# Two edits to a one-core transformer kernel: preparation moved between the first three stages, and a query's squares folded before they are summed

## The chip, the cores and the metric

The kernel runs on one core of a Trainium2 chip. The metric is the device time of one execution in microseconds (us). The engines of the core are TensorE (PE in the rows, with PEld for its weight loads), VectorE (DVE), ScalarE (ACT), GpSimd (POOL) and SyncE (SP), which here only issues transfers. Each works through its own instructions in order, and they wait for one another on semaphores.

## The reference

`x` and `ctx` are [8, 256, 512] in float32. Two layers, each an attention and a feed-forward block, are added to `x`:

```python
x = x + xattn0(layernorm(x), ctx)      # one head of 512; keys = [ctx ; x wk], values = [ctx ; x wv]
x = x + ffn0(layernorm(x))             # ternary weights, 8-bit activations
x = x + xattn1(layernorm(x), ctx)      # 16 query heads of 128, 4 key/value groups, keys only from ctx
x = x + moe(layernorm(x))              # top 2 of 8 experts and a shared expert

# ffn0: every weight matrix is rounded with one scale of its own
gamma_w = clip(mean(abs(w)), 1e-5);  w_dq = clip(round(w / gamma_w), -1, 1) * gamma_w
gamma_x = clip(max(abs(x), -1), 1e-5); x_dq = clip(round(x * 127 / gamma_x), -128, 127) * gamma_x / 127

# xattn1: every query head and key head is divided by its own root mean square
q = rmsnorm(x @ Wq + bq);  k = rmsnorm(ctx @ Wk + bk);  v = ctx @ Wv + bv
p = softmax(q k^T / sqrt(128) + mask);  out = (p v) @ Wo
```

## The kernel before, in words

`program` (L2612) runs five stages. The first two are functions of their own, the third and fourth share one function and one block, and the fifth is not touched by the change. A float32 product is made as three products of float32r halves: each operand is split in a high part, written by ACT (a copy that rounds), and a low part, the difference, written by DVE or POOL; `matmul3` (L76) issues the three.

**First attention, `attention0` (L161).** Eight turns, one for a batch of 256 rows. In turn i, PE makes the scores of batch i, the queries and keys of batch i+1, the transposed probabilities, the output, the values of batch i+1 and the projection. The turns are hardware loops (`Fori`) on PE, ACT, POOL and SP. At its end SP loads the key weights of the second attention and the first context tiles into `ahead`.

**Keys, values and ternary weights, `keys_values_ternary` (L540).** Sixteen tiles of 128 context rows. PE makes keys(t), the transposed keys of tile t-1, and values(t). Around it lies the preparation of the ternary weights: 24 pieces of 128x1024, of three matrices. ACT takes the absolute values with their sums (`absolute`, L699), DVE and PE make the mean of a matrix (`scale_of`, L762; `inverse_of`, L766), then ACT scales each piece (`scaled`, L703) and DVE rounds it (`ternary`, L773). `measured`, `averaged` and `rounded` (L594 to L597) say at which tile which piece has its turn: four pieces in each of six tiles. Ahead of tile 0 the weights of keys and values are split (L708, L713, L787, L794) and the gate bias is cut in six bf16 rows on DVE (L792 to L800). DVE also takes the layernorm statistics of all 16 row tiles (L782). POOL writes the low parts of the context and stores keys and values (L651, L653), and at the end waits until both have landed (L667).

**First feed-forward block and second attention, `ffn0_attention1` (L864).** The block begins with the biases' loads, the norm of the first four row tiles, their scales and the first quantised tile (L1422 to L1430); then 16 steps of up, gate and down products.

The second attention has 64 units: four groups of heads, in each four pairs of batches, in each four heads. Order on each engine in iteration u:

- PE: the sums of squares of unit u+2 (`square_sums`, L1577; behind the transposes, or ahead of them where u is a multiple of four), the transposed probabilities of u, the query product of u+3, the scores of u+2, the output of u, and after every fourth unit a projection of 48 products (`project`, L1633). I call four units and their projection a cluster.
- ACT: `transposed` of u (L1209), `exp` of u+1 (L1202), `queries` of u+3 (L1192: squares, then the high part of the query), `output` of u.
- DVE: the sums' copy of u+2 (L1372), the low parts of the transposed probabilities of u, `normalise` of u+1 (L1392), `scores` of u+2 (L1376: times 1/rms, plus mask), the query's low part of u+3, `maxima` of u+2 (L1386), `output` of u (L1406).
- POOL: `rstd` of u+2 (L1062: the power -1/2), and now and then low parts of weights, keys and values.

`exp` of a unit waits for its `maxima`; `normalise` for its `exp`; `scores` on DVE for the `rstd` and for PE's scores. The squares are summed over the 128 lanes by four products a unit, each with a 128x128 tile of squares as weights and one column of ones:

```python
for t in range(CT):    # L1582
    last = pe.matmul(ssb[:, t:t + 1], sq[i % 2][:, t * P:(t + 1) * P], ones[:, 0:1], start=True, stop=True)
```

Of the kernel before, what the change touches and what calls it, by code (L numbers as in the profile page):

```python
# [6 lines left out]
ALU = mybir.AluOpType  # L7
# [143 lines left out]
def layernorm_stats(dve, ctx_sems, X, stats, mv, tiles):  # L151

    s_stats, s_mv = ctx_sems
    for t in range(tiles):
        dve.bn_stats(stats[:, t, :], X[:, t, :]).then_inc(s_stats, 1)
    for t in range(tiles):
        dve.wait_ge(s_stats, at(t + 1))
        dve.bn_aggr(mv[:, t, :], stats[:, t, :]).then_inc(s_mv, 1)


def attention0(nc, banks, X, eps, ident, x_dram, ctx_dram, ctxT_dram, w_dram, B, S, ahead, wk1_dram):  # L161
# [5 lines left out]
    with Phase(nc, 1) as ctx:  # L167
        def sb(name, shape, dt=F32):
            return ctx.enter_context(nc.sbuf_tensor("a0_" + name, shape, dt))

        def sem(name):
            return ctx.semaphore("a0_" + name)

        def pair(name, shape):
            return Pair(ctx, nc, "a0_" + name, shape)
# [4 lines left out]
        W = [pair(n, [P, KD, D]) for n in ("wq", "wk", "wv", "wo")]  # L180
        wq, wk, wv, wo = W
        wraw = [sb(f"wraw{j}", [P, KD, D]) for j in range(2)]
        stats = sb("stats", [P, QT, 6])
        mv = sb("mv", [P, QT, 2])
        ve, rstd, mhalf = (sb(n, [P, QT]) for n in ("ve", "rstd", "mhalf"))
        xn = sb("xn", [P, QT, D])
        xT = pair("xT", [P, KD, S])
        qT = pair("qT", [P, KD, S])
        kT = pair("kT", [P, KD, 2 * S])
        V = pair("V", [P, KT, D])  # L190
        cTraw = sb("cTraw", [P, KD, S])
        craw = sb("craw", [P, QT, D])
        probs = sb("probs", [P, QT, 2 * S])
        pT = pair("pT", [P, KT, S])
        oT = pair("oT", [P, KD, S])
        nmax = sb("nmax", [P, QT])
        den = sb("den", [P, QT])
        rden = sb("rden", [P, QT])
        bank = banks
# [12 lines left out]
        s_proj, s_added = sem("projected"), sem("added")  # L212

# [3 lines left out]

        @block.sync  # L220
        def _(sp):
            sp.dma_start(X[:, 0:QT, :], x_dram[:, 0:QT, :]).then_inc(s_x[0], 16)
# [5 lines left out]
            for j in (2, 3):  # L228
                sp.wait_ge(s_wlo, at(j - 1))
                sp.dma_start(wraw[j - 2][:], w_dram[j]).then_inc(s_w[j], 16)  # L230
            sp.dma_start(X[:, 2 * QT:T, :], x_dram[:, 2 * QT:T, :]).then_inc(s_x[2], 16)
            with sp.Fori(1, B) as i:
                sp.wait_ge(s_cTlo, at(i))
                sp.dma_start(cTraw[:], ctxT_dram[:, :, bass.ds(i * S, S)]).then_inc(s_cT, 16)
                sp.wait_ge(s_clo, at(i))
                sp.dma_start(craw[:], ctx_dram[:, bass.ds(i * QT, QT), :]).then_inc(s_c, 16)
            sp.dma_start(ahead.raw[:], wk1_dram).then_inc(ahead.raw_loaded, 16)
            sp.dma_start(ahead.ctx[:], ctxT_dram[:, :, 0:S]).then_inc(ahead.ctx_loaded, 16)

        @block.gpsimd  # L240
        def _(pool):
            def context(i):

                pool.wait_ge(s_cThi, at(i + 1))
                pool.tensor_tensor(kT.lo[:, :, 0:S], cTraw[:], f32(kT.hi[:, :, 0:S]), ALU.subtract).then_inc(s_cTlo, 1)
                pool.wait_ge(s_chi, at(i + 1))
                pool.tensor_tensor(V.lo[:, 0:QT, :], craw[:], f32(V.hi[:, 0:QT, :]), ALU.subtract).then_inc(s_clo, 1)

            def inverse(k):

                pool.wait_ge(s_ve, at(k + 1))
                pool.tensor_tensor(rstd[:], ve[:], mhalf[:], ALU.pow).then_inc(s_rstd, 1)

            pool.memset(mhalf[:], -0.5).then_inc(s_half, 1)
            pool.wait_ge(s_half, at(1))
            inverse(0)
            pool.wait_ge(s_cThi, at(1))
            pool.tensor_tensor(kT.lo[:, :, 0:S], cTraw[:], f32(kT.hi[:, :, 0:S]), ALU.subtract).then_inc(s_cTlo, 1)
            inverse(1)
            pool.wait_ge(s_chi, at(1))  # L260
            pool.tensor_tensor(V.lo[:, 0:QT, :], craw[:], f32(V.hi[:, 0:QT, :]), ALU.subtract).then_inc(s_clo, 1)
            pool.wait_ge(s_whi, at(4))
            pool.tensor_tensor(wo.lo[:], wraw[1][:], f32(wo.hi[:]), ALU.subtract).then_inc(s_wolo, 1)
            with pool.Fori(1, B - 1) as i:
                inverse(i + 1)
                context(i)
            context(B - 1)

        @block.scalar
        def _(act):  # L270
            def weights(j):
                act.wait_ge(s_w[j], at(16))
                act.activation(W[j].hi[:], wraw[j % 2][:], ACT.Copy).then_inc(s_whi, 1)

            def transposed_x(i):
                for t in range(QT):
                    act.wait_ge(tr.mm, at(i * QT + t + 1))
# [3 lines left out]
            def context_keys(i):  # L281

                act.wait_ge(s_cT, at(i * 16 + 16))
                act.activation(kT.hi[:, :, 0:S], cTraw[:], ACT.Copy).then_inc(s_cThi, 1)

            def context_values(i):
                act.wait_ge(s_c, at(i * 16 + 16))
                act.activation(V.hi[:, 0:QT, :], craw[:], ACT.Copy).then_inc(s_chi, 1)

            def projected(i, f, dst, b0, scale):  # L290
                for m in range(2):
                    act.wait_ge(f.mm, at(i * 2 + m + 1))
# [9 lines left out]
            def values(i):  # L302
                for t in range(QT):
                    act.wait_ge(v.mm, at(i * QT + t + 1))
                    act.activation(V.hi[:, QT + t, :], bank[6 + t][:], ACT.Copy).then_inc(v.hi, 1)

            def turn(i, more):
                if more:
                    transposed_x(i + 1)
                for t in range(QT):  # L310
                    act.wait_ge(s_nmax, at(i * QT + t + 1))
                    act.activation(probs[:, t, :], bank[t][:], ACT.Exp, bias=nmax[:, t:t + 1],
                                   accum_out=den[:, t:t + 1]).then_inc(s_exp, 1)
                if more:
                    queries(i + 1)
                    context_keys(i + 1)
                for t in range(QT):
                    act.wait_ge(pt.mm, at(i * QT + t + 1))
                    act.activation(pT.hi[:, :, t * P:(t + 1) * P],
                                   bank[4 + t][:].rearrange("p (k s) -> p k s", k=KT), ACT.Copy).then_inc(pt.hi, 1)  # L320
                if more:
                    keys(i + 1)
                for m in range(2):
                    act.wait_ge(o.mm, at(i * 2 + m + 1))
                    if m == 0:
                        act.wait_ge(s_proj, at(i * QT))
# [16 lines left out]
            with act.Fori(0, B - 1) as i:  # L343
                turn(i, True)
            turn(B - 1, False)
# [2401 lines left out]
```

## Time and profile before

| what | value |
|---|---|
| runs before | 1871.54 us median of 3 (1871.28 to 1875.71) |
| profiled execution | 1874.65 us, span 1872.9 us |
| busy share of the span | PE 94%, PEld 77%, DVE 66%, ACT 45%, POOL 30% |
| mean granted TensorE clock | 0.97 |
| first attention | 3.6 to 309.7 us |
| keys, values, ternary weights | 310.7 to about 454 us |
| first feed-forward block | 455 to about 709 us, with the second attention's first units at its end |
| second attention | 709 to 1363 us |
| last stage | 1363 to 1872.9 us |

How to read it: PE is busy nearly everywhere, and the stretches where it is not lie at the borders of the second stage. The stages run one after the other, so what a stage gains or loses goes into the end one for one. Times in rows are us from the span's start.

### The profile page before, as it was taken

To read this page: it belongs to the slowest core of one execution; us is meant where nothing else is said; L and a number is where in the kernel's file an instruction comes from. 1 tells how busy PE (TensorE), PEld (TensorE's weight loads), DVE (VectorE), ACT (ScalarE), POOL (GpSimd) and SP (SyncE) were. 2 spreads that over 40 slices of the span, in tenths; PEclk is the share of its full clock that TensorE was granted. 3 is DMA by queue.
4 is the path that set the end of the run, shared out by engine and by line. 5 is a ranking of instruction groups with operands and counts; after the bars stand their busy time and mean duration, and the time that the engine had idled before them with its cause. 6 is when DMAs were issued, how large, how long until landed. Compare 5 with 4: busy or idle time off the path is not lost. (4 is left out here: it accounts for less than half of the span.)

```text
span 1872.9 us, 26972 instructions
## 1 busy us (share of the span) xinstructions
PE 1752.1 (94%) x9950; PEld 1449.3 (77%) x9970; DVE 1237.4 (66%) x2357; ACT 852.0 (45%) x1621; POOL 558.8 (30%) x408
## 2 busy tenths in 40 slices
PE   6999996884799989999999999999889999999999
PEld 6988995763344458888888888888756789999876
DVE  4444433776789857677777767778666567676655
ACT  3222321674455545455555445555332256555411
POOL 2111111221666632122221212221120145464342
PEclk9999998997899998999999999999989999999999
DMA  6110113464122374122221212220053288888573
GB/s 224 34 34 22 34 45 109 153 223 145 23 68 70 88 208 145 57 93 90 89 80 57 79 57 86 95 68 1 1 193 116 88 279 277 281 279 269 194 251 107
DMA packets 160946, 225.38 MB, mean 120 GB/s; under 512 B 41655, under 2 KB 101303, under 8 KB 158647
## 3 DMA queue, kind: packets, MB, share of 16 engines
q1 hardware_dynamic: 150940, 189.50, 30.5%
q0 software_dynamic: 9888, 34.35, 5.8%
q8 instruction: 70, 1.15, 0.3%
q14 instruction: 48, 0.39, 0.1%
HBM read 171.65 MB, written 43.78 MB: 115 GB/s over the span
## 5 line engine op out<-in xcount | busy, mean ns | idle before, releaser
L1065 POOL TENSOR_TENSOR a_rq<-a_ssq,a_qhalf 128x4 f32<-128x4 f32 x64 | 65.1, 1017 | 404.2 <-DVE a_ssq L1374 404.2
L1212 ACT ACTIVATE a_pT_hi<-bank 128x512 fp32r<-128x512 f32 x128 | 69.5, 598 | 185.4 <-PE bank L1614 185.4
L78 PE MATMUL bank<-a_xT_hi,a_wq_lo 128*128 128x512 f32 (+1 forms) x384 | 144.7, 377 | 6.8 <-issue 3.7
L1206 ACT ACTIVATE a_scores<-a_scores,a_nmax 128x256 f32<-128x256 f32 x256 | 127.2, 504 | 27.5 <-DVE a_nmax L1389 27.3
L79 PE MATMUL bank<-a_xT_lo,a_wq_hi 128*128 128x512 f32 (+1 forms) x384 | 139.0, 362 | 0.0
L80 PE MATMUL bank<-a_xT_hi,a_wq_hi 128*128 128x512 f32 (+1 forms) x384 | 138.8, 362 | 0.0
L78 PE MATMUL bank<-a_wo_hi,a_oT_lo 128*128 128x512 f32 x320 | 127.1, 397 | 3.1 <-DVE a_oT_lo L416 1.5
L79 PE MATMUL bank<-a_wo_lo,a_oT_hi 128*128 128x512 f32 x320 | 125.3, 391 | 0.0
L1382 DVE SCALAR_TENSOR_TENSOR a_scores<-bank,a_rq,a_mask 128x256 f32<-128x256 f32 x256 | 106.1, 477 | 28.7 <-PE bank L80 20.4
L80 PE MATMUL bank<-a_wo_hi,a_oT_hi 128*128 128x512 f32 x320 | 125.0, 391 | 0.0
L1924 POOL TENSOR_TENSOR e_wg_lo<-raw_g,e_wg_hi 128x1408 fp32r<-128x1408 f32 x26 | 91.3, 3511 | 112.8 <-ACT e_wg_hi L1991 112.8
L1099 POOL TENSOR_TENSOR f_h<-f_vv,f_gs 128x512 f32<-128x512 f32 x64 | 95.4, 1492 | 79.1 <-DVE f_vv L1319 77.7
L78 PE MATMUL bank<-a_pT_hi,a_V_lo 128*128 128x256 f32 x384 | 110.4, 288 | 7.9 <-DVE a_pT_lo L1403 6.3
L1414 DVE TENSOR_TENSOR X<-X,bank 128x512 f32<-128x512 f32 x64 | 43.7, 687 | 101.0 <-PE bank L80 101.0
L80 PE MATMUL bank<-a_pT_hi,a_V_hi 128*128 128x256 f32 x384 | 109.4, 285 | 0.0
L79 PE MATMUL bank<-a_pT_lo,a_V_hi 128*128 128x256 f32 x384 | 109.3, 285 | 0.0
L1403 DVE TENSOR_TENSOR a_pT_lo<-bank,a_pT_hi 128x512 fp32r<-128x512 f32 x128 | 82.1, 682 | 18.1 <-ACT a_pT_hi L1212 18.0
L1398 DVE TENSOR_SCALAR a_scores<-a_scores,a_rden 128x256 f32<-128x256 f32 x256 | 85.9, 399 | 2.3
L78 PEld LDWEIGHTS bank<-a_xT_hi,a_wq_lo 128*128 128x128 f32 x384 | 74.3, 194 | 16.7 <-issue 7.6
L80 PEld LDWEIGHTS bank<-a_xT_hi,a_wq_hi 128*128 128x128 f32 x384 | 74.0, 193 | 11.4
L79 PEld LDWEIGHTS bank<-a_xT_lo,a_wq_hi 128*128 128x128 f32 x384 | 74.9, 195 | 8.9
L78 PEld LDWEIGHTS bank<-a_pT_hi,a_V_lo 128*128 128x128 f32 x384 | 74.2, 193 | 9.7 <-DVE a_oT_lo L1408 6.9
(404 smaller groups left out, 5350.5 us busy)
## 6 DMA issues: line engine op xcount, KB each, us to landing
raw_g<-in_egw SPq DMA_DIRECT2D x26, 704.0 KB, 4.8
raw_u<-in_euw SPq DMA_DIRECT2D x26, 704.0 KB, 6.2
a_xT_hi<-x1T_hi SPq DMA_DIRECT2D x16, 1024.0 KB, 6.0
a_xT_lo<-x1T_lo SPq DMA_DIRECT2D x16, 1024.0 KB, 8.3
raw_d<-in_edw SPq DMA_DIRECT2D x26, 512.0 KB, 5.7
y_routed<-m_y SPq DMA_DIRECT2D x39, 256.0 KB, 6.8
raw_d<-in_edw SPq DMA_DIRECT2D x26, 192.0 KB, 6.6
a_cTraw<-in_ctxT SPq DMA_DIRECT2D x8, 512.0 KB, 3.5
```

The costliest lines, as they stand in the source:

```text
L78: pe.matmul(out, w[1], x[0], start=first, stop=False)
L79: pe.matmul(out, w[0], x[1], start=False, stop=False)
L80: return pe.matmul(out, w[0], x[0], start=False, stop=last)
L1065: pool.tensor_tensor(rq[:, h % HG, :], ssq[:, h % HG, :], qhalf[:], ALU.pow).then_inc(s_rq, 1)
L1099: pool.tensor_tensor(h[n % 2][:, j * 512:(j + 1) * 512], vv[u % 2][:], gs[u % 2][:], ALU.mult).then_inc(s_h, 1)
L1206: act.activation(row, row, ACT.Exp, bias=nmax[:, i % 2, t:t + 1], accum_out=den[:, i % 2, t:t + 1]).then_inc(s_exp, 1)
L1212: act.activation(pT[b].hi[:], ptb[b][:].rearrange("p (k s) -> p k s", k=QT), ACT.Copy).then_inc(ft.hi, 1)
L1382: dve.scalar_tensor_tensor(sc[i % 2][:, r, :], scb[b][:, t * S:(t + 1) * S], rq[:, i % HG, r:r + 1], mask[:, t, :], ALU.mult, ALU.add).the ...
L1398: dve.tensor_scalar(row, row, rden[:, i % 2, t:t + 1], None, ALU.mult).then_inc(s_p, 1)
L1403: dve.tensor_tensor(pT[b].lo[:], ptb[b][:].rearrange("p (k s) -> p k s", k=QT), f32(pT[b].hi[:]), ALU.subtract).then_inc(ft.lo, 1)
L1414: dve.tensor_tensor(row, row, ptb[t % 2][:], ALU.add).then_inc(s_added, 1)
L1924: pool.tensor_tensor(pairs[w % 2].g.lo[:], raws[raw_of(w)].g[:], f32(pairs[w % 2].g.hi[:]), ALU.subtract).then_inc(s_glo, 1)
```

## The change

**Between the first three stages.** (1) The absolute values of the 24 pieces, their sums and the three scales move into the first attention: SP loads four pieces a turn in turns 0 to 5, ACT takes them between its copies, DVE and PE make all three scales in the last two turns. So the pieces are loaded a second time in the second stage, where only `scaled` and `ternary` are left, two pieces a tile in tiles 1 to 12. (2) The weights of keys and values and the first two context tiles are split at the end of the first attention, and the gate rows are cut there, all low parts on POOL. (3) The layernorm statistics of a batch are taken one turn later in the first attention; two tiles are left for the second stage. (4) In the second stage PE transposes the keys of tile t-2 instead of t-1, and the normed key goes to another buffer, so that two waits fall. (5) The norm, scales and quantisation of the first four row tiles (two quantised), the feed-forward biases and constants move from the third stage into the second. (6) The second stage no longer waits for its last stores; SP waits for them in the third stage before it loads from them. (7) The hardware loops of the first attention are written out.

**In the second attention.** ACT squares a query in four instructions of 64 lanes x 256 columns, which write the two batches of a pair to two halves of the lanes; POOL adds the two halves of the columns (`fold`); PE sums by two products a unit with two columns (`batch`), one for each half of the lanes.

```diff
 # attention0, ACT, in each turn (absolute does nothing from piece 24 on)
+            def absolute(n):
+                w, c = n // keep.chunks, n % keep.chunks
+                if n < PIECES:
+                    act.wait_ge(s_piece[n % PER], n // PER * 16 + 16)
+                    act.activation(pieces[n % PER], pieces[n % PER], ACT.Abs,
+                                   accum_out=keep.asum[:, w, c:c + 1]).then_inc(s_abs, 1)
...
                     context_keys(i + 1)
+                    absolute(i * PER)
...
+                    absolute(i * PER + 1)
                     keys(i + 1)
+                    absolute(i * PER + 2)
...
                     values(i + 1)
+                    absolute(i * PER + 3)
 # attention0, SP, in turn i
+                for n in range(i * PER, min((i + 1) * PER, PIECES)):
+                    if i:
+                        sp.wait_ge(s_abs, n - PER + 1)
...
+                    piece(n)
 # keys_values_ternary, PE
-            pe.wait_ge(s_wlo, 1)
-            for t in range(T):
+            for t in range(T - 1):
                 keys(t)
-                if t >= 1:
-                    transposed(t - 1)
...
+                if t >= 2:
+                    transposed(t - 2)
+                if t < T - 2:
+                    values(t)
+            keys(T - 1)
+            transposed(T - 3)
+            values(T - 2)
+            values(T - 1)
+            transposed(T - 2)
             transposed(T - 1)
 # keys_values_ternary, DVE
+            for t in range(T):
+                cs = rounded.get(t, range(0))
+                biased(t)
                 if t >= 1:
                     values_out(t - 1)
+                summed(t)
+                for n in cs[0:1]:
+                    ternary(n)
+                normed(t)
+                for n in cs[1:2]:
+                    ternary(n)
...
 # ffn0_attention1, POOL
+            def fold(u, i):
+                pool.wait_ge(s_sq, u * 4 + 4)
+                pool.tensor_tensor(sq[i % 2][:, 0:S], sq[i % 2][:, 0:S], sq[i % 2][:, S:2 * S], ALU.add).then_inc(s_fold, 1)
...
+            fold(0, 0)
+            fold(1, 1)
             rstd(0, 0)
+            fold(2, 2)
             rstd(1, 1)
             for u in range(G * U):
                 g, i, n = u // U, u % U, u // HG
+                if u + 3 < G * U:
+                    fold(u + 3, i + 3)
                 if u + 2 < G * U:
                     rstd(u + 2, i + 2)
 # ffn0_attention1, ACT, queries
-                act.activation(sq[i % 2][:], qb[i % 2][:], ACT.Square, bias=b).then_inc(s_sq, 1)
+                for n, lanes in enumerate((slice(0, P // 2), slice(P // 2, P))):
+                    for m, to in enumerate((slice(0, P // 2), slice(P // 2, P))):
+                        act.activation(sq[i % 2][to, (n ^ m) * S:((n ^ m) + 1) * S], qb[i % 2][lanes, m * S:(m + 1) * S],
+                                       ACT.Square, bias=bqg[g % 2][lanes, i % HG:i % HG + 1]).then_inc(s_sq, 1)
                 act.activation(q[i % 2].hi[:], qb[i % 2][:], ACT.Identity, bias=b).then_inc(fq.hi, 1)
 # ffn0_attention1, PE, square_sums
-                pe.wait_ge(s_sq, u + 1)
+                pe.wait_ge(s_fold, u + 1)
...
-                for t in range(CT):
-                    last = pe.matmul(ssb[:, t:t + 1], sq[i % 2][:, t * P:(t + 1) * P], ones[:, 0:1], start=True,
-                                     stop=True)
+                for t in range(QT):
+                    last = pe.matmul(ssb[:, t:t + QT + 1:QT], sq[i % 2][:, t * P:(t + 1) * P], batch[:], start=True, stop=True)
```

## Rows read from the trace of the kernel before

**Rows 1.** Busy time in three stretches: PE, PEld, DVE, ACT, POOL, clock, DMA share, GB/s.

```profile
3.00:309.70 306.70, 289.67 (x1856) 262.88 (x1856) 128.63 (x203) 91.03 (x149) 50.25 (x26) 0.99 0.17 60
309.70:465.30 155.60, 108.90 (x465) 86.28 (x466) 108.55 (x206) 90.97 (x146) 36.41 (x43) 0.84 0.54 189
...
709.20:1363.00 653.80, 645.73 (x4012) 574.70 (x4012) 482.25 (x1093) 334.49 (x858) 140.65 (x106) 0.99 0.21 70
```

**Rows 2.** Timeline, DVE, SP and PE, into the second stage: start, us, engine, line.

```profile
308.98 0.75 DVE L428 SCALAR_TENSOR_TENSOR X<-bank,a_rden,X 128x512 f32<-128x512 f32 x1 [2.00 <-PE bank L80]
...
310.73 0.35 SPq L618 DMA_DIRECT2D kv_vst<-in_gb  x1
...
316.26 0.76 PE L78 MATMUL bank<-kv_wk_hi,kv_cT_lo 128*128 128x512 f32 x1 [7.31 <-POOL kv_cT_lo L646]
```

**Rows 3.** What PE waited for, 310 to 455 us: total, times, longest.

```profile
PE bank L838 <- DVE kv_kf L752: 14.8, 6, 3.8
```

**Rows 4.** Timeline, PE, into the third stage.

```profile
443.01 0.66 PE L838 MATMUL bank<-ident,kv_kf 128*128 128x128 f32 x4 [3.84 <-DVE kv_kf L752]
...
465.30 1.91 PE L1544 MATMUL bank<-f_wg,f_xqT 128*128 128x512 bf16 x4 [0.34 <-issue]
```

**Rows 5.** Timeline of one tile of the second stage: PE, then DVE, then POOL.

```profile
356.98 0.60 PE L838 MATMUL bank<-ident,kv_kf 128*128 128x128 f32 x4
362.92 0.60 PE L838 MATMUL bank<-ident,kv_kf 128*128 128x128 f32 x4
...
357.18 0.69 DVE L742 TENSOR_TENSOR kv_kf<-bank,kv_bk 128x512 f32<-128x512 f32 x1 [1.75 <-PE bank L80]
...
360.43 0.43 DVE L779 TENSOR_SCALAR f_wg<-f_wg 128x1024 bf16<-128x1024 bf16 x1
...
361.59 0.69 DVE L782 BATCH_NORM_STATS2 kv_stats<-X 128x6 f32<-128x512 f32 x1
...
362.41 1.60 DVE L777 TENSOR_SCALAR f_wg<-kv_ring 128x1024 bf16<-128x1024 f32 x1
...
362.17 1.29 POOL L646 TENSOR_TENSOR kv_cT_lo<-kv_cTraw,kv_cT_hi 128x512 fp32r<-128x512 f32 x1 [4.37 <-ACT kv_cT_hi L680]
```

**Rows 6.** The first ternary operation (L777) of one matrix: count, then least, median, greatest ns.

```profile
L777 DVE TENSOR_SCALAR f_wg<-kv_ring x8: 685/694/1599, 359.7 to 375.1; 128x1024 bf16<-128x1024 f32 x8
```

**Rows 7.** Timeline, PE, in the second attention, from one cluster to the next.

```profile
998.22 0.95 PE L1583 MATMUL bank<-ones,a_sq 128*128 128x1 f32 x8
...
1013.17 1.04 PE L1614 MATMUL bank<-ident,a_scores 128*128 128x128 f32 x8
...
1020.56 1.04 PE L1614 MATMUL bank<-ident,a_scores 128*128 128x128 f32 x8
...
1039.26 0.95 PE L1583 MATMUL bank<-ones,a_sq 128*128 128x1 f32 x8
```

**Rows 8.** What POOL and DVE waited for, 709.2 to 1363 us: total, times, longest.

```profile
POOL a_rq L1065 <- DVE a_ssq L1374: 397.0, 55, 15.8
...
DVE a_scores L1382 <- POOL a_rq L1065: 5.9, 7, 0.9
```

**Rows 9.** Timeline of one unit of the second attention: DVE, then ACT.

```profile
973.14 1.66 DVE L1382 SCALAR_TENSOR_TENSOR a_scores<-bank,a_rq,a_mask 128x256 f32<-128x256 f32 x4 [0.93 <-POOL a_rq L1065]
...
975.37 1.27 DVE L1389 TENSOR_REDUCE a_nmax<-a_scores 128x2 f32<-128x512 f32 x2
976.56 0.68 DVE L1408 TENSOR_TENSOR a_oT_lo<-bank,a_oT_hi 128x512 fp32r<-128x512 f32 x1
...
976.08 0.51 ACT L1206 ACTIVATE a_scores<-a_scores,a_nmax 128x256 f32<-128x256 f32 x1 [2.45 <-DVE a_nmax L1389]
...
978.07 0.67 ACT L1199 ACTIVATE a_sq<-bank,a_bqg 128x512 f32<-128x512 f32 x1
```

**Rows 10.** Timeline, PE and POOL, at the second attention's entry in the third stage.

```profile
693.12 0.95 PE L1583 MATMUL bank<-ones,a_sq 128*128 128x1 f32 x8
...
695.88 1.02 POOL L1065 TENSOR_TENSOR a_rq<-a_ssq,a_qhalf 128x4 f32<-128x4 f32 x1
```

More of the change, by code:

```diff
@@ L166, in attention0 @@
     SCALE = float(D) ** -0.5
-    with Phase(nc, 1) as ctx:
-        def sb(name, shape, dt=F32):
-            return ctx.enter_context(nc.sbuf_tensor("a0_" + name, shape, dt))
+    NR = 6
+    N = len(f_dram)
+    CH = keep.chunk
+    PIECES = N * keep.chunks
+    PER = 4
+    with Phase(nc) as ctx:
         def sem(name):
             return ctx.semaphore("a0_" + name)
-        def pair(name, shape):
-            return Pair(ctx, nc, "a0_" + name, shape)
         def flow(name):
             return Flow(ctx, nc, "a0_" + name)
[L180 to L184, printed above, removed]
-        ve, rstd, mhalf = (sb(n, [P, QT]) for n in ("ve", "rstd", "mhalf"))
[L186 to L199, printed above, removed]
@@ new lines, in attention0 @@
+        low, mid, high = Region(nc, low), Region(nc, mid), Region(nc, high)
+        wo = low.pair("a0_wo", [P, KD, D])
+        kT = low.pair("a0_kT", [P, KD, 2 * S])
+        V = low.pair("a0_V", [P, KT, D])
+        xn = low.take("a0_xn", [P, QT, D])
+        wq, wk, wv = (high.pair("a0_" + n, [P, KD, D]) for n in ("wq", "wk", "wv"))
+        probs = [r.take(f"a0_probs{j}", [P, 2 * S]) for j, r in enumerate((mid, high))]
+        W = [wq, wk, wv, wo]
+        xT, qT = mid.pair("a0_xT", [P, KD, S]), mid.pair("a0_qT", [P, KD, S])
@@ L201, in attention0 @@
+        fstats = sb("fstats", [P, QT, 6])
+        assert QT == 2 and mid.offset <= keep.high and high.offset <= keep.limit
+        pieces = [wraw[k // 2][:].rearrange("p k n -> p (k n)")[:, k % 2 * CH:(k % 2 + 1) * CH] for k in range(PER)]
+        grow = wraw[1][0:NR, :, :].rearrange("p k n -> p (k n)")
+        gb6 = keep.gb6
+        bank, tot = banks, banks[6]
         s_x = [sem(f"x{j}_loaded") for j in range(3)]
@@ L342, in _ @@
             values(0)
-            with act.Fori(0, B - 1) as i:
+            for i in range(B - 1):
                 turn(i, True)
+            act.wait_ge(ahead.raw_loaded, 16)
+            act.wait_ge(q.mm, 2 * B)
+            act.activation(kv.wk.hi[:], ahead.raw[:], ACT.Copy).then_inc(s_kvhi, 1)
+            act.wait_ge(s_wv1, 16)
+            act.wait_ge(k.mm, 2 * B)
+            act.activation(kv.wv.hi[:], wraw[0][:], ACT.Copy).then_inc(s_kvhi, 1)
             turn(B - 1, False)
@@ new lines, in keys_values_ternary @@
+        mem = Region(nc, keep.base)
+        kst, vst = mem.take("kv_kst", [P, 2, G, S]), mem.take("kv_vst", [P, 2, QT, D])
+        kf = [mem.take(f"kv_kf{j}", [P, G, HD]) for j in range(2)]
+        ksq = [mem.take(f"kv_ksq{j}", [P, G, HD]) for j in range(2)]
+        bk = mem.take("kv_bk", [P, D])
+        assert mem.offset <= keep.area
+        mem = Region(nc, keep.area)
+        ring = [mem.take(f"kv_ring{j}", [P, CH]) for j in range(RING)]
+        assert mem.offset <= keep.high
+        mem = Region(nc, kv.end)
@@ L629, in _ @@
-            for b in (2, 3, 4):
-                context(b)
-            for c in half(0):
-                chunk(1, c)
-            context(5)
-            for c in half(4):
-                chunk(1, c)
-            for b in (6, 7):
-                context(b)
-            for c in range(NCH):
-                chunk(2, c)
+            piece(0)
+            piece(1)
+            context(2)
+            for n in range(2, RING):
+                piece(n)
+            context(3)
+            for n in range(RING, PIECES):
+                piece(n)
+                if n >= 10 and n % 4 == 2:
+                    context(n // 4 + 2)
@@ L871, in ffn0_attention1 @@
     KH = H // P
-    GROUPS = [(0, 1), (1, 4)] + [(t, t + 4) for t in range(4, T, 4)]
     GT = 4
+    GROUPS = [(t, t + GT) for t in range(0, T, GT)]
+    READY = 2
     XS = 2 * GT
@@ L908, in ffn0_attention1 @@
         K = [first.K, over.pair("a1_K", [P, C])]
+        V = [first.V, over.pair("a1_V", [P, CT, HD])]
+        over = Region(nc, prep.end)
         oT = over.pair("a1_oT", [P, HG, C])
         pT = [over.pair(f"a1_pT{b}", [P, QT, S]) for b in range(NB)]
-        V = [first.V, over.pair("a1_V", [P, CT, HD])]
         wo = over.pair("a1_wo", [P, HG, D])
```

664 lines of the change are left out of this document (356 added, 308 removed).

## The prediction

> **What bounds the kernel now.** I read the busy shares first, then windows by stage, then the waits inside a window, then timelines at the places that the change touches. The windows show one picture: in the first attention PE is busy 289.67 of 306.7 us, in the second 645.73 of 653.8, both at full clock; only from 309.7 to 465.3 is it idle for 46.7 us, at a mean clock of 0.84 [rows 1]. So time can be won between the first and the third stage without PE doing less, and elsewhere only by taking work from PE, or be lost by making it wait. The reader is to see where the idle part lies. PE enters the second stage with a wait of 7.31 us for POOL's low part, after the phase has started at 310.73 [rows 2]; six times it waits for the normed key, 14.8 us together [rows 3], once more at 443.01, and its first up product starts at 465.30, four of them taking 1.91 us [rows 4]. In the second attention the timeline repeats in clusters of 1039.26 - 998.22 = 41.04 us, with 1020.56 - 1013.17 = 7.39 a unit [rows 7], so the closing unit with its 48 products takes 41.04 - 3 x 7.39 = 18.87, and one product (18.87 - 7.39) / 48 = 0.239.
>
> **Part one, the first attention.** It gains work: on ACT 24 pieces of 128x1024, at most twice a 0.67-us row each [rows 9], 32 us beside 91.03 busy; on DVE the statistics, 16 rows of 0.69 with their aggregates; on POOL the gate rows, four passes over 2048 elements or 16 x 1.29 = 21 us [rows 5] in the seventh turn, and two weights' low parts. PE has 289.67 us of its own in these 306.7 and none of the others comes near: ACT 123, DVE 145, POOL about 50 + 35 [rows 1]. The one queue risk is POOL's last context behind the gate rows; a turn is some 36 us, 21 + 3 fit in it. Cover gone, the price would be the part beyond the turn, some us once. I take 0. Writing the loops out I cost at 0 too: PE has nowhere an idle moment there that a loop's branch would explain.
>
> **Part two, the second stage.** Before: 465.30 - 310.73 = 154.6 us from the phase's start to the first up product. After, term by term. PE can start with the phase: what it waited 7.31 us for is now made before. A tile by PE's own pace is 362.92 - 356.98 = 5.94 [rows 5], and 16 of them 95.0; the three-buffer key and the transposes of tile t-2 remove the waits of [rows 3]. Does DVE let PE keep that pace? In the tile shown it needs 361.59 - 357.18 = 4.41 for biases, sums, norm and one ternary pair, and a second pair costs 0.69 [rows 6] + 0.43 = 1.1 [rows 5]: 5.5, the statistics being gone. That is under 5.94, by 0.4 only. ACT has two 128x1024 scalings and four smaller rows a tile, about 2 x 1.3 + 3 x 0.67 = 4.6. Then the tail: PE's last transposes wait for the last norm, 2.0; the quantisation of two row tiles and the last keys and values on ACT and DVE, some five rows of 0.69, 3.6; phase border 310.73 - 309.73 = 1.0 [rows 2]; two transposes of a quantised tile with their copies, 2.5. Sum 104.1; saved 50.5. For a half-clock start and an odd collision I give back 2: **-48**. The bounds: DVE binds (rival C), -39; the tail half as long and a full-clock start to the ups (1.91 falls to 1.0), -56.
>
> The stores that are no longer waited for land during the third stage's start, beside its loads; the DMA share was 0.54 in the old stretch [rows 1], and the pieces, loaded twice, add 12.6 MB in the first attention, where the share is 0.17. No cost.
>
> **Part three, the squares.** Removed: half of PE's four sums a unit, 0.95 to 0.475 [rows 7]; over 64 units 30 us of PE work. Added on ACT: four squares of 64 lanes by 256 columns in place of one of 128x512 that took 0.67 [rows 9]; lanes run side by side, so each lies between 0.67 / 2 = 0.34 and the 0.51 of the 256-column exponential [rows 9]. I take the middle, 1.7 for the four. Added on POOL: an addition of 128x256, between half of 1.29 [rows 5], 0.65, and all of it; I take 0.70, near half, since the work is elementwise.
>
> Now the order. On POOL fold(u+3) stands ahead of rstd(u+2). The fold waits for the squares of u+3, which on ACT stand behind exp(u+1), which waits for maxima(u+1). And rstd(u+2), queued behind the fold, is waited for by DVE's scores(u+2), behind which stands maxima(u+2). That closes a loop of one unit, which before did not exist: rstd needed only sums that PE had made early. Round the loop:
> maxima to exp 976.08 - 975.37 = 0.71; four exponentials 978.07 - 976.08 = 1.99; squares 1.7; fold 0.70; power 1.02 [rows 10] and a signal, 1.04; scores to maxima 975.37 - 973.14 = 2.23 [rows 9]. Sum **8.37 us**, against 7.39 by PE before and 6.9 by PE now. The loop binds; PE waits for the rest. The waits of before agree that there is no room: DVE's scores waited for POOL 7 times, up to 0.9 us [rows 8], although POOL had nothing ahead of the power.
>
> A cluster then takes 3 x 8.37 = 25.1 and the closing unit, whose loop runs through PE: scores to the output's low part 976.56 - 973.14 = 3.42, that part 0.68 [rows 9]; the 30 of 48 products that need it 7.2; sums 0.48; transposes 1.04 [rows 7] and 0.5 for the last addition; the query product, 12 x 0.239 + 0.2 = 3.07; squares 1.7, fold 0.7, power 1.04. Sum 19.8. Cluster 44.9, that is 3.9 more than 41.04, or 62 over 16. Where POOL also has a weight's low part in its queue (seven clusters, four times 1.29 and its load's issue) I add 1 each, and take 2 off for the last cluster, which has no successor: **+67**. At the entry PE's first sums came at 693.12, while POOL stood idle until the norm of the last row tile and its power at 695.88 [rows 10]; fold(0) is queued behind that norm, so the sums start near 696.7: **+3**. Bounds: squares 0.34 and fold 0.65 give a loop of 7.98, clusters of 43.4, 46 in all; squares 0.51 and fold 1.29 give 9.3 and 130.
>
> **Sum.** -48 + 67 + 3 = +22 on the profiled execution's 1874.65 us (span 1872.9), 1896.6. The median shown lies 3.1 lower, so I predict 1871.5 + 22 = 1893 us.
>
> **Rivals.** A, on the other side: PE stays the bound in the second attention. Speaking for it: POOL waited 397 us there for DVE's sums [rows 8], so it has room by its busy time; against it, what counts is the order of its queue. Then -48 - 30 = -78: 1793. It needs the loop under 6.9, which even the lowest bounds (7.98) do not give; only if the squares were not behind the exponentials. B: the loop binds, but is shorter. Each 0.1 us off it takes 0.4 off a cluster, 6.4 in all; at 8.37 - 22 / 64 = 8.03 the change is worth nothing, and that is the squares at their lower bound. Below it lies 1850 to 1871. C: DVE becomes the bound of the second stage. Where POOL's 1.29-us low part ran, the ternary operation took 1.60 instead of 0.69 [rows 5, 6]; if this meets every tile, DVE needs 5.5 + 0.9 = 6.4, with the second operation caught too 6.8; (6.8 - 5.94) x 12 = 10 us, 1903. For it: the low part of the context comes once a tile, and there are now two pairs a tile for it to meet; against it: of eight rows the median was 0.694. D: the granted clock, now 0.99 through the second attention [rows 1], falls in the new gaps of PE of 1 to 2 us a unit. Four half-clock products took 1.91 us at 465.30 after some 20 us of little work, nearly twice their time; if a stretch of 3.4 us a cluster went at half clock, 16 x 1.7 = 27 us more, up to 1920. Against it: all gaps now there are short and leave it at 0.99.
>
> Of C the Trainium skill has a rule (SBUF — State Buffer, Who interferes with whom): VectorE and GpSimd share one pair of ports, an exclusive lock; a DVE instruction in a two-port mode and a GpSimd one block each other fully, whoever issues first. By that rule the ternary operation waits out whatever of the 1.29 us is left, and the trace agrees with its 1.60. It also says that a two-input DVE operation contends with GpSimd's reads when both inputs lie in SBUF; the scores read a bank, so by the rule the fold would not slow them, and the sum stands.
>
> **How the numbers follow.** The forecast (1878 to 1911, loop 8.1 to 8.6) gets 0.62, A 0.08, B 0.14, C 0.10, D 0.06. A measurement of this kernel tells about 0.3%, 5.6 us, from no change. A is faster, B half faster and half within, C and D slower, and the forecast's own lower edge gives a little to within: faster 0.16, same 0.08, slower 0.76. The range goes from 1856, which leaves out A and the low end of B, to 1922, which leaves out only the dear folds.
>
> **What the profile of the changed kernel should show.** Right: PE's first product of the second stage within 1 us of the phase's start; no wait for the normed key longer than 1 us but at the end; 104 us from the phase's start to the first up product; ternary pairs of 1.1 us. In the second attention four records of the sums in 0.48 us; squares near 0.42 apiece and a fold near 0.70; POOL's fold waiting for ACT's squares; DVE's scores waiting for POOL's power 1 to 2 us in every unit; PE idle some 6 us a cluster, 8.4 a unit, 45 a cluster. The last stage should keep its 510 us. Wrong: if DVE's scores wait for PE instead of POOL, the loop does not bind and A or B holds; if PE's idle time in the second stage stays, ahead of transposes or of values, C holds; if the clock of a second-attention slice is under 0.95, D. The forecast falls most easily by the price of four short squares, since 0.1 us on each moves the time by 26.

## The result, and the profile after

The changed kernel takes 1947.3 us (1943.82 to 1951.25, 4 runs) against 1871.41 beside it: a ratio of 1.0402, interval 1.0374 to 1.043, slower by 76 us. The direction was forecast, the size was not: 1893 was predicted, and 1947 lies above the range. The profiled execution took 1949.32 us with a span of 1947.6, 74.7 more than before.

The windows of the changed kernel (first attention; second stage up to the first up product; second attention; columns as in [rows 1]) and then what its engines waited for between 709 and 1435 us:

```profile
3.00:311.88 308.88, 291.65 (x1858) 265.68 (x1858) 138.18 (x234) 119.02 (x201) 75.81 (x34) 0.99 0.31 105
311.88:428.62 116.74, 100.45 (x459) 81.00 (x460) 89.47 (x151) 61.28 (x94) 30.57 (x40) 0.93 0.68 231
709.00:1435.00 726.00, 634.53 (x3606) 540.80 (x3606) 467.59 (x1049) 384.81 (x990) 171.23 (x158) 0.96 0.17 55
```

```profile
POOL a_sq L1172 <- ACT a_sq L1323: 525.2, 53, 20.4
ACT a_pT_hi L1337 <- PE bank L1725: 227.2, 22, 15.9
DVE a_scores L1504 <- POOL a_rq L1177: 113.9, 59, 2.6
```

The first attention took the added work at no cost in time: PE is busy 291.65 of 308.88 us. The second stage went from 154.57 to 116.74. In the second attention PE's idle share rose from 1% to 13%, and the forecast wait is there: DVE's scores waited 59 times for POOL's power, 113.9 us, where before it was 7 times and 5.9 us [rows 8]. Above it stands the fold waiting for the squares, which before did not exist.

Now the timeline of one plain unit, DVE, ACT, POOL (the answer to [rows 9]):

```profile
1092.21 1.66 DVE L1504 SCALAR_TENSOR_TENSOR a_scores<-bank,a_rq,a_mask 128x256 f32<-128x256 f32 x4 [2.06 <-POOL a_rq L1177]
...
1094.45 1.27 DVE L1511 TENSOR_REDUCE a_nmax<-a_scores 128x2 f32<-128x512 f32 x2
...
1100.91 1.66 DVE L1504 SCALAR_TENSOR_TENSOR a_scores<-bank,a_rq,a_mask 128x256 f32<-128x256 f32 x4 [2.07 <-POOL a_rq L1177]
...
1095.16 0.51 ACT L1331 ACTIVATE a_scores<-a_scores,a_nmax 128x256 f32<-128x256 f32 x1 [2.59 <-DVE a_nmax L1511]
...
1097.14 1.94 ACT L1323 ACTIVATE a_sq<-bank,a_bqg 64x256 f32<-64x256 f32 x4
...
1099.16 0.74 POOL L1172 TENSOR_TENSOR a_sq<-a_sq 128x256 f32<-128x256 f32 x1 [6.98 <-ACT a_sq L1323]
1099.86 1.02 POOL L1177 TENSOR_TENSOR a_rq<-a_ssq,a_qhalf 128x4 f32<-128x4 f32 x1
```

Follow it round: scores at 1092.21, maxima 1094.45, exponentials 1095.16, squares 1097.14, fold 1099.16, power 1099.86, the next scores 1100.91. That is 8.70 us. Each step starts at the end of the one before it, but for the maxima: between them and the scores stands DVE's low part of the next query, 0.74 us. Nothing in this chain is PE's.

The closing unit, on PE, from one cluster's sums to the next:

```profile
1017.93 0.50 PE L1695 MATMUL bank<-a_batch,a_sq 128*128 128x2 f32 x4
...
1056.77 0.50 PE L78 MATMUL bank<-a_wo_hi,a_oT_lo 128*128 128x512 f32 x1 [2.17 <-DVE a_oT_lo L1530]
1057.11 0.39 PE L79 MATMUL bank<-a_wo_lo,a_oT_hi 128*128 128x512 f32 x1
1057.34 0.49 PE L80 MATMUL bank<-a_wo_hi,a_oT_hi 128*128 128x512 f32 x1
1057.63 0.63 PE L78 MATMUL bank<-a_wo_hi,a_oT_lo 128*128 128x512 f32 x1
1058.06 0.63 PE L79 MATMUL bank<-a_wo_lo,a_oT_hi 128*128 128x512 f32 x1
...
1060.62 0.53 PE L79 MATMUL bank<-a_wo_lo,a_oT_hi 128*128 128x512 f32 x1
1060.99 0.39 PE L80 MATMUL bank<-a_wo_hi,a_oT_hi 128*128 128x512 f32 x1
...
1065.31 0.50 PE L1695 MATMUL bank<-a_batch,a_sq 128*128 128x2 f32 x4
```

The cluster is 1065.31 - 1017.93 = 47.38 us, against 41.04 [rows 7]; those with more on POOL took 48.3. PE waits 2.17 us for the last output, works on, and 0.9 us later its products stand 0.43 us apart instead of 0.23, until about 1060.8. The granted clock between 1057.60 and 1060.80 is 0.50, the lower of the two levels (1.2 of 2.4 GHz). These products are on the loop's way; the run filled_gap below shows that their slowness is not hidden.

Last, the end of the second stage: PE, DVE, POOL (the answer to [rows 4]):

```profile
410.48 0.60 PE L957 MATMUL bank<-ident,kv_ksq 128*128 128x128 f32 x4
416.63 1.11 PE L957 MATMUL bank<-ident,kv_ksq 128*128 128x128 f32 x4 [5.55 <-DVE kv_ksq L856]
425.85 0.59 PE L1636 MATMUL bank<-f_identb,f_xq 128*128 128x128 bf16 x4 [8.11 <-PEq L56]
...
409.27 2.28 DVE L887 TENSOR_REDUCE f_ax<-f_xn 128x4 f32<-128x2048 f32 x1
...
413.24 0.69 DVE L846 TENSOR_TENSOR kv_kf<-bank,kv_bk 128x512 f32<-128x512 f32 x1
...
420.09 0.76 POOL L767 DMA_DIRECT2D K<-kv_kst  x1
425.81 0.10 POOL L1160 MEMSET f_mhalf<- 128x1 f32 x1 [4.96 <-POOLq L56]
```

Before the last tile's bias DVE has the moved absolute maximum and ten small rows, and PE waits 5.55 us; and the border to the third stage takes 4.96 us after the issue of POOL's last store.

Where the 74.7 us are, from the ends of the stages and the starts of POOL's powers (695.88 to 1337.86 before, 664.91 to 1413.65 after):

| part | forecast | measured |
|---|---|---|
| first attention, to the start of the second stage | 0 | +1.1 |
| second stage, to the first up product | -48 | -37.8 |
| first up product to the first power | +3 | +5.7 |
| first to last power | +67 | +106.8 |
| after it | 0 | -1.1 |
| sum | +22 | +74.7 |

The first line is no effect: in the profiled executions of this study the second stage started between 307.99 and 311.88 us, in kernels of either kind.

### The profile page after: what moved, and what is told of

The parts are those of the page before. It is cut to its first block and busy times, and to the rows that moved or that the text cites. A ratio compares the mean times of both kernels' runs of the same rounds, so it can differ in the third digit from the quotient of the medians.

```text
span 1947.6 us, 26472 instructions
## 1 busy us (share of the span) xinstructions
PE 1759.3 (90%) x9690; PEld 1435.0 (74%) x9710; DVE 1233.1 (63%) x2334; ACT 926.4 (48%) x1813; POOL 625.4 (32%) x480
## 5 line engine op out<-in xcount | busy, mean ns | idle before, releaser
L1172 POOL TENSOR_TENSOR a_sq<-a_sq 128x256 f32<-128x256 f32 x64 | 47.5, 742 | 551.9 <-ACT a_sq L1323 551.9
L78 PE MATMUL bank<-a_wo_hi,a_oT_lo 128*128 128x512 f32 x320 | 135.9, 425 | 34.3 <-DVE a_oT_lo L1530 32.8
L79 PE MATMUL bank<-a_wo_lo,a_oT_hi 128*128 128x512 f32 x320 | 134.1, 419 | 0.0
L80 PE MATMUL bank<-a_wo_hi,a_oT_hi 128*128 128x512 f32 x320 | 133.5, 417 | 0.0
L1323 ACT ACTIVATE a_sq<-bank,a_bqg 64x256 f32<-64x256 f32 x256 | 119.7, 468 | 17.0 <-PE bank L80 12.2
L78 PEld LDWEIGHTS bank<-a_pT_hi,a_V_lo 128*128 128x128 f32 x384 | 74.7, 195 | 47.1 <-DVE a_oT_lo L1530 34.6
L78 PEld LDWEIGHTS bank<-a_wo_hi,a_oT_lo 128*128 128x128 f32 x320 | 64.8, 202 | 57.4 <-DVE a_oT_lo L1530 39.1
L1520 DVE TENSOR_SCALAR a_scores<-a_scores,a_rden 128x256 f32<-128x256 f32 x256 | 91.1, 419 | 2.3
L1725 PE MATMUL bank<-ident,a_scores 128*128 128x128 f32 x512 | 71.7, 281 | 19.2 <-DVE a_scores L1520 12.6
```

Of the source, the lines that this page charges most:

```text
L78: pe.matmul(out, w[1], x[0], start=first, stop=False)
L79: pe.matmul(out, w[0], x[1], start=False, stop=False)
L80: return pe.matmul(out, w[0], x[0], start=False, stop=last)
L1323: act.activation(sq[i % 2][to, (n ^ m) * S:((n ^ m) + 1) * S], qb[i % 2][lanes, m * S:(m + 1) * S], ACT.Square, bias=bqg[g % 2][lanes, i % ...
L1520: dve.tensor_scalar(row, row, rden[:, i % 2, t:t + 1], None, ALU.mult).then_inc(s_p, 1)
L1725: last = pe.transpose(ptb[b][:, k * S + t * P:k * S + (t + 1) * P], sc[i % 2][:, r, k * P:(k + 1) * P], ident[:])
```

## The experiments

Clusters are worked out in all runs as in [rows 7], from the starts of the sums behind a projection; "plain" is the usual value of the others, of which the last one or two differ in some runs, and "weights" are the seven clusters in which POOL also makes a low part of wq or wo.

| run | us | ratio to before, interval | clusters: plain / weights |
|---|---|---|---|
| before | 1871.4 | | 41.0 / 41.2 |
| changed | 1947.3 | 1.0402 (1.0374 to 1.043) | 47.4 / 48.3 |
| shifts_only | 1838.1 | 0.9819 (0.9802 to 0.9835) | 41.0 / 41.2 |
| fold_only | 1984.4 | 1.0593 (1.0576 to 1.0611) | 47.4 / 48.2 |
| swap | 1862.9 | 0.9953 (0.9937 to 0.997) | 39.7 / 45.6 |
| one_square | 1864.2 | one run | 41.4 / 43.4 |
| swap_split | 1832.4 | 0.978 (0.9755 to 0.9805) | 39.7 / 40.4 |
| filled_gap | 1934.4 | 1.0317 (1.0293 to 1.0342) | 46.2 / 47.0 |
| few_context_lo | 1939.0 | one run | 47.4 / 48.3 |
| sp_store | 1942.8 | one run | 47.4 / 48.3 |
| late_context_hi | 1952.9 | one run | 47.4 / 48.3 |
| shifts_tuned | 1842.5 | 0.9829 (0.981 to 0.9849) | 41.0 / 41.2 |
| all_tuned | 1833.7 | 0.9791 (0.9773 to 0.9808) | 39.7 / 40.4 |
| best | 1826.0 | 0.9754 (0.9728 to 0.978) | 39.7 / 40.4 |

### Each part alone

`shifts_only` is the changed kernel with the old squares, and `fold_only` the old kernel with the new ones. Of the first one's edit, the part on ACT (the fold goes and PE's four products come back as well):

```diff
...
-                for n, lanes in enumerate((slice(0, P // 2), slice(P // 2, P))):
-                    for m, to in enumerate((slice(0, P // 2), slice(P // 2, P))):
-                        act.activation(sq[i % 2][to, ...], qb[i % 2][lanes, m * S:(m + 1) * S], ACT.Square, ...)
+                act.activation(sq[i % 2][:], qb[i % 2][:], ACT.Square, bias=b).then_inc(s_sq, 1)
```

> The changed kernel with the squares and their sums of before: one square of 128x512, four products, no fold. It keeps all the shifts of the first three stages. Theory (the two parts are independent; the shifts won 37 us up to the first up product): 1834 to 1838. Rival (the moved loads or buffers also slow the second attention or the last stage): above 1850, with clusters longer than 41.1.

> The kernel before with only the fold: four squares, the addition on POOL, two products a unit. Theory (the fold alone costs 107 us in the loop and 4 at the entry): 1978 to 1986. Rival (part of the loss comes from the shifts): under 1965.

1838.1 and 1984.4: both theories hold, the first at the edge of its range. -35 and +111 us add to 76, which is the whole change, so the parts add. Everything that was lost was lost by the fold.

### The order of POOL's queue

```diff
-                if u + 3 < G * U:
-                    fold(u + 3, i + 3)
                 if u + 2 < G * U:
                     rstd(u + 2, i + 2)
+                if u + 3 < G * U:
+                    fold(u + 3, i + 3)
```

> The changed kernel, with POOL's power of unit u+2 ahead of its fold of unit u+3; nothing else differs. Theory (the order of POOL's queue closes the loop): DVE's scores no longer wait behind the squares, a unit falls from 8.69 us to 7.4 or less and a cluster from 47.9 to between 39.1 and 41.1, so 107 to 140 us are won and the time is 1806 to 1840. Rival (the added work on ACT and POOL itself, or PE's clock, is what costs): a unit stays above 8.3 and the time above 1920.

84 us less, same work, but 1863 is between the two forecasts. Plain clusters take 39.7, as the theory said; those with weights 45.6. PE, DVE and POOL in one of those:

```profile
948.32 0.44 PE L1725 MATMUL bank<-ident,a_scores 128*128 128x128 f32 x2 [1.33 <-DVE a_scores L1520]
949.91 1.01 PE L1695 MATMUL bank<-a_batch,a_sq 128*128 128x2 f32 x4 [1.16 <-POOL a_sq L1172]
...
945.26 3.00 DVE L1520 TENSOR_SCALAR a_scores<-a_scores,a_rden 128x256 f32<-128x256 f32 x4
...
941.07 4.63 POOL L1181 TENSOR_TENSOR a_wq_lo<-ahead_raw,a_wq_hi 128x2048 fp32r<-128x2048 f32 x1 [1.78 <-ACT a_wq_hi L1294]
...
949.14 0.72 POOL L1172 TENSOR_TENSOR a_sq<-a_sq 128x256 f32<-128x256 f32 x1
```

The loop is gone, but PE now depends on a fold in every unit, and POOL has a 4.63-us operation, a load, a key's low part and a power ahead of it. The normalisation on DVE took 3.00 instead of 1.14 beside POOL's work. After PE's waits of 1.33 and 1.16 its sums took 1.01 instead of 0.50, and the granted clock between 950 and 952 is 0.50: the lower level again. `swap_split` cuts the weights' low parts in quarters over three units:

```diff
-                if i == 0:
-                    wo_lo(g)
-                if i == U // 2 and g + 1 < G:
-                    wq_lo(g + 1)
+                if i < 3:
+                    wo_lo(g, QUARTERS[i])
+                if U // 2 <= i < U // 2 + 3 and g + 1 < G:
+                    wq_lo(g + 1, QUARTERS[i - U // 2])
```

> The kernel of the run swap, in which seven clusters of sixteen took 45.6 us and most others 39.7; here POOL's low parts of wq and wo are cut in quarters, one in each of two units and two in the third, so that no fold or power waits behind 4.6 us at once. Theory (in those seven clusters PE waits for a fold and for a normalisation behind the long low part, and the half clock after it): all clusters near 39.7 and 7 x 5.9 = 41 us less, 1820 to 1828. Rival (any low part on POOL holds up DVE's normalisation as much): 1850 or more.

Clusters with weights fell from 45.6 to 40.4 and the time by 30 us, to 1832.4: that the long low part is the cause is shown, though not how much came through the fold and how much through the normalisation. The forecast was 4 us too low, since 0.7 us a cluster stayed and the first cluster (44.1) gained less.

The fold takes 30 us of work from PE, and beside shifts_only, which lacks it, this kernel gains some 6 us, hardly clear of noise. A plain cluster is 1.3 us shorter and not 1.8, since PE now has a gap of 0.44 us in it; the clusters with weights and the last two gained less or nothing.

### The loop's length

```diff
-                for n, lanes in ...:
-                    for m, to in ...:
-                        act.activation(...).then_inc(s_sq, 1)
+                act.activation(sq[i % 2][:], qb[i % 2][:], ACT.Square, bias=b).then_inc(s_sq, 4)
```

> The changed kernel with one square of 128x512 in place of the four, so the fold adds the wrong halves and the root mean squares of the queries are wrong; order, fold and two products stay. Theory (the loop's length sets the time): the loop loses 1.96 - 0.57 = 1.39 us, a unit takes 7.3, a closing unit 19.9 or, with PE's full clock back, 18.5; cluster 41.8 or 40.4, time 1850 or 1828. Rival (the fold or POOL's place in the chain costs more than its own time): above 1870.

A unit took 7.50 us and a closing unit 18.94, cluster 41.4; 1864 lies between the forecasts. The loop lost 1.19 us, 0.2 less than its one shortened step, and POOL's low parts stretched the seven clusters to 43.4. So four squares instead of one cost about 80 of the 111 us. Of the 6.0 us that a cluster lost here, 4.8 are four turns of the shorter loop, and the rest is in the closing unit, where PE's gap is 0.97 us instead of 2.17 and the granted clock stays at 1.00. The squares cost through the loop and through the gap that it makes: in the run swap, where the loop is broken, the same four squares are there and plain clusters are shorter than before.

### The clock

Nine discarded products fill the gap ahead of the projection's last head:

```diff
+                        if t0 == 0 and len(heads) > 1:
+                            pe.wait_ge(fo.lo, u)
+                            for k in heads:
+                                matmul3(pe, ptb[0][:], part(oT, slice(None), k, slice(0, P)), part(wo, slice(None), k),
+                                        k == 0, k == HG - 2)
```

> The changed kernel with nine more products of PE a cluster, ahead of the projection: the first group is made once, thrown away and made again, 2.06 us of work in a gap of 2.17. Theory (the granted clock falls after that gap and lengthens the closing unit by 1.5 us): the closing stretch runs at full clock, a cluster takes 46.3 instead of 47.8, 24 us less in all, 1920 to 1927. Rival (the clock falls for another reason, or the stretch is not on the loop's path): 1943 to 1951.

1934.4, with clusters 1.25 us shorter. One cluster in this run, then in the changed kernel:

```profile
1022.50:1068.60 46.10, 42.89 (x251) 36.35 (x249) 29.46 (x67) 26.88 (x68) 13.80 (x12) 1.00 0.16 52
```

```profile
1022.50:1070.50 48.00, 42.83 (x246) 36.49 (x246) 29.75 (x70) 25.61 (x69) 9.38 (x10) 0.96 0.17 56
```

The clock is at 1.00, though PE still has gaps of 0.85 us in other units. More work made the kernel faster, and the clock is shown to be on the loop's way; but 1934.4 lies between the two forecasts. The clusters gained 1.25 us each, 20 in all, where the forecast had 24 and took the whole slow stretch as won; and the medians differ by 13 only. Some of the gain is lost behind the last power: from there to the projection's last product it is 28.9 us instead of 24.0. Why is not shown.

### The second stage

> The changed kernel; in the second stage, from context tile 6 on, POOL makes the low part of only one of 128 columns, so the rest of the low part is that of an older tile. Theory (each tile's second ternary operation takes 1.40 instead of 0.43 because POOL's low part runs beside it, and so DVE sets the tile at 6.46): it takes 0.43, a tile takes 5.94 by PE, and the first up product comes 5 us sooner. Rival (DVE's pace is set by its waits for ACT, 0.45 and 0.46 a tile): tiles stay at 6.4.

```diff
-                pool.tensor_tensor(cT[t % 3].lo[:], src, f32(cT[t % 3].hi[:]), ALU.subtract).then_inc(s_clo, 1)
+                w = P if t < 6 else 1
+                pool.tensor_tensor(cT[t % 3].lo[:, :, 0:w], src[:, :, 0:w], f32(cT[t % 3].hi[:, :, 0:w]),
+                                   ALU.subtract).then_inc(s_clo, 1)
```

The second ternary operation of one matrix in the changed kernel, then here (count, least, median, greatest ns):

```profile
L872 DVE TENSOR_SCALAR f_wo<-f_wo x8: 426/914/1414, 378.3 to 399.6; 128x1024 bf16<-128x1024 bf16 x8
```

```profile
L874 DVE TENSOR_SCALAR f_wo<-f_wo x8: 426/427/428, 371.5 to 390.1; 128x1024 bf16<-128x1024 bf16 x8
```

One of the two operations a tile took 1.4 us, now none. In the changed kernel PE's transposes stood 5.93 us apart up to 362.87 and 6.46 from 369.03 on; here 5.93 to the last ternary tile. The first up product comes 109.35 us after the stage's start instead of 116.74, so 7.4 us sooner, more than the 5 expected. Only 2.9 of them are in the tiles. The other 4.5 are in the tail, on PE:

```profile
406.31 0.66 PE L959 MATMUL bank<-ident,kv_ksq 128*128 128x128 f32 x4 [1.08 <-DVE kv_ksq L858]
```

DVE has the same maximum and the same ten small rows ahead of the last tile's bias here, but PE waits 1.08 us and not 5.55: without the collisions DVE needs 5.5 us a tile and comes to the tail ahead of PE; with them it comes late, and PE waits there for the lag that DVE has gathered.

`sp_store` moves the last two stores from POOL to SP:

```diff
 # POOL
-            store(B - 1)
 # SP
...
+            sp.wait_ge(s_vf, (b + 1) * QT)
+            sp.dma_start(v_dram[:, b * QT:(b + 1) * QT, :], vst[:, j, :, :]).then_inc(stored[2], 16)
+            sp.wait_ge(s_kev, (b + 1) * QT)
+            sp.dma_start(k_dram[:, :, b * S:(b + 1) * S], kst[:, j, :, :]).then_inc(stored[2], 16)
```

> The changed kernel with the last two stores of keys and values issued by SP in place of POOL. The border between the second and the third stage took 5.0 us after POOL's last store. Theory (the border waits for POOL's own queue of stores): the border falls to 1.7, as between the first two stages, and the first up product comes 3 us sooner. Rival (it waits for any landing, or for something else): it stays between 4 and 5.5.

Its border, on SP and PE:

```profile
418.32 0.64 SPq L758 DMA_DIRECT2D K<-kv_kst  x1
420.27 0.41 SPq L1121 DMA_DIRECT2D ahead_raw<-in_Wq  x1
...
420.32 0.59 PE L1640 MATMUL bank<-f_identb,f_xq 128*128 128x128 bf16 x4 [3.95 <-PEq L56]
```

1.3 us from the end of the last issue to the next stage; 112.79 us from the stage's start to the first up product. The landings say what the border waits for. With the stores in POOL's queue the next stage began 1.62 us after the last of them had landed (424.19 in the changed kernel), and by the same 1.62 in few_context_lo, swap and shifts_only. Here it began at 420.27, before SP's last store had landed at 422.64, and 1.83 after the landing of the last store that POOL still issues. So the border held for stores in POOL's queue and not for SP's.

`late_context_hi` moves ACT's rounding of the next context tile:

```diff
 # ACT, in tile t
                 squares(t)
+                if 1 <= t and t + 2 < T:
+                    context_hi(t + 2)
...
-                if t + 3 < T:
-                    context_hi(t + 3)
```

> The changed kernel; in the second stage ACT rounds the next context tile right behind a tile's squares instead of at the tile's end, so POOL's low part starts some 4 us later, beside DVE's reduction. Theory (the collision with the second ternary operation sets the pace of 6.46 from the seventh tile on): that operation stays at 0.43, the tiles are between 5.9 and 6.1, the first up product comes 3 to 5 us sooner after the phase's start than 116.7. Rival (moving it makes ACT or the first ternary operation late by as much): 116 or more.

The forecast missed. The long operations are gone (0.43), but DVE's longest waits are now others:

```profile
DVE kv_vst L864 <- DMA K<-kv_kst: 14.9, 5, 5.1
```

POOL's stores stand behind the low part that now comes late, so the staging buffers come free late; the first up product came 122.9 us after the stage's start, 6 us later. A collision was traded for a queue.

> The run shifts_only, with the context rounded as in late_context_hi and the last two stores issued by SP as in sp_store; squares and sums as before the change. Theory (both gains add): 4 + 4 us under shifts_only, 1828 to 1832. Rival (they hide one another): 1834 or more.

> The run swap_split, with the context rounded as in late_context_hi, the last two stores by SP, and the first fold ahead of the last row tile's norm on POOL. It differs from shifts_tuned only in the fold and POOL's order. Theory (with the queue in order the fold is worth 1.3 us in most clusters and 0.6 in seven, less what the entry keeps): 1832 - 8 - 3, 1819 to 1824, and 6 to 12 us under shifts_tuned. Rival (the fold is worth nothing in itself): within 3 us of shifts_tuned.

Both round the context late, as late_context_hi does, and both missed: 1842.5 where 1828 to 1832 was forecast, on the rival's side, and 1833.7 where it was 1819 to 1824. They show no gain over shifts_only and swap_split: the ratios overlap (0.9829 with 0.9819, 0.9791 with 0.978). Between the two the fold, with POOL's queue in order, is worth 8.8 us of medians, as forecast, and the intervals of the ratios just part (0.981 and 0.9808). The last run has the context rounded where the changed kernel has it:

> The run all_tuned with the rounding of the context back at the tile's end, where the changed kernel has it: swapped and cut POOL queue, last two stores by SP, first fold ahead of the last norm. Theory (in late_context_hi the later low part pushed POOL's stores back, and DVE and PE waited for the staging buffers they free; without it the gains of sp_store, 4, and of the entry, 3, stand): the first up product 112.8 us after the phase's start, 1824 to 1829 in all. Rival (the gains at the two borders are taken back by what follows them): 1831 or more.

1826.0 us, a ratio of 0.9754: as forecast, with 112.93 us to the first up product, and the lowest median of all. Its interval overlaps that of swap_split, so the gain over that kernel, 3.7 us up to the first up product by the traces, is not clear of noise in the whole time.

## Why the prediction was wrong

The loop, the wait that closes it and the parts that gain were forecast rightly; what failed is sizes, all in one direction, and the place given to two rivals. Of the 53 us between +22 and +74.7, the squares are 20, PE's clock behind its gap 20, the second stage 10 and the entry 3.

- **The loop through POOL's queue** (shown by swap). Forecast 8.37 us a unit, measured 8.70. Of its terms only the squares were off: 1.7 was the middle between 0.34 and 0.51 each; they took 1.94 for four and 0.08 to the fold, near the upper bound. 0.32 x 4 x 16 = 20 us. The fold (0.70 from start to power) and the rest stood as worked out.
- **The closing unit.** Forecast 19.8, measured 1073.93 - 1052.62 = 21.31 from scores to scores. The squares account for 0.3, and the products behind PE's gap for up to 1.4: they were summed at 0.239 each, and seven or so took 0.43. That is rival D, with its 1.7 a cluster, put aside at 0.06 because no gap of before had brought the clock down; filled_gap puts it at 1.25 a cluster, 20 us. Its stretch of 3.4 us at half clock was taken from no row; it measured 3.2, and the nearness is luck.
- **The second stage.** 104.1 forecast (106 with the allowance), 116.7 measured. Rival C is there, and few_context_lo shows its cause and its price, 7.4 us where the forecast had put 10: one of the two second operations of a tile is caught every time, so DVE needs 6.46 and not 5.5, and PE pays 2.9 us in the tiles and 4.5 in the tail, where it waits 5.55 us instead of the 2.0 forecast. The row of before with 1.60 had pointed at it. And the border was taken as the one between the first two stages, 1.0; it was 5.0, since it held until POOL's stores had landed. That the wait for them had been taken out of the code said nothing of the border, 4 us.
- **The entry.** +5.7 instead of +3: PE waited 4.9 us for the first fold.
- **The first attention** cost nothing, as forecast, and the last stage kept its 510 us (from the last product of the second attention to the end 509.9, before 510.0).
- **The step that failed most** is the combination. C and D were rivals with chances of their own, so each was priced on top of the forecast by itself. But neither excludes the forecast: the loop makes the very gaps that D needs. Forecast, C and D together, by the numbers written down, make 22 + 10 + 27 = +59, within 16 of the measurement and outside the range.
- **Rival A** names the better kernel, but not its price: swap_split, with the order in POOL's queue turned round and the long operation cut, has clusters of 39.7 us, within one gap of 0.44 of PE's own work. Its 1832 is far from A's 1793, since the second stage gained 38 us and not 48, and the fold 6 to 9 and not 30.

## What to carry to other kernels

When work is added to an engine with much idle time, ask not how long it is but what stands behind it in that engine's queue, and walk the ring that it closes; one line's order was worth 84 us here. Rivals that follow from the forecast (a gap, then a lower clock) are added to it and not weighed against it. And when an engine falls behind in a stage's loop, look for the price in the stage's tail as well, and price a border by the transfers that are still under way.

## What the runs showed of the hardware

- A square of 64 lanes x 256 columns frees ACT after 0.49 us (changed kernel), a 128x512 one after some 0.57 (one_square): a quarter of the elements, nearly the same time.
- After PE had waited 2.17 us in a stream of work its products went to 0.43 us apart, 0.9 us later, for 3.2 us, at a granted clock of 0.50; with that gap filled, others of 0.85 us left the clock at 1.00, and so did one of 0.97 in one_square. After waits of 1.33 and 1.16 close together (swap) it was at 0.50 again.
- DVE's 128x1024 operation from bf16 to bf16 took 0.43 us alone and 1.41 beside POOL's 1.29-us low part. The Trainium skill (SBUF — State Buffer, Who interferes with whom) says that a DVE operation in a two-port mode, which one like this can enter, and one of GpSimd block each other fully; the trace agrees, 393.11 + 1.40 ending just after POOL's 392.94 + 1.29, and few_context_lo has 0.43 where the low part is gone.
- A border between stages lasted 4.96 us after the issue of stores from POOL's queue, 1.62 after they had landed, and 1.3 after the issue of the same stores from SP's, which landed 2.4 us after it was over.
